# Two layer-norm stages of a fused two-layer kernel: statistics issued ahead of the tile's matmul pipe, and their sums taken by fp32 matmuls

## The reference

```python
# x = x + layernorm(L0_attn(layernorm(x)))
x_norm = _layernorm(x, ln1_g, ln1_b)
beta = x_norm @ w_in.T                              # 1024 -> 2 x 64
c_r, c_i = _chunked_eigenstate(log_decay, frequency, beta_r, beta_i)   # scan in chunks of 64
c_r = einsum('hjk,bthk->bthj', coupling, c_rh)      # 4 heads of 16 x 16, and the same for c_i
h = concat([c_r, c_i]) @ w_out.T
gate = sigmoid(x_norm @ w_gate.T + b_gate)
x1 = residual + gate * h
x2n = _layernorm(x1, ln2_g, ln2_b)
mlp = silu(x2n @ w_mlp1.T + b_mlp1) @ w_mlp2.T + b_mlp2   # 1024 -> 4096 -> 1024
return x1 + mlp
```

## Time and profile before

| | |
|---|---|
| runs of the kernel before | 9948.44 and 10145.99 us, median 10047.22 |
| the profiled execution | 9851.24 us |
| its span, slowest core (core 5) | 9849.6 us; the 8 cores 9819.1 to 9849.6 |
| busy in the span | PE 4153.1, PEld 2035.3, DVE 2423.2, ACT 1759.9, POOL 779.8 us |
| mean granted TensorE clock | 0.699 of 2.4 GHz |
| stages by time | L1A to about 1590 us, L1B to 3860, then L2A 5110, L2B 6210, L3 8655, L4 |

### The profile page before, as it was taken

The page is one execution under the profiler, slowest core; times in us unless marked ns, Lnnn a source line. Parts: engine busy times, 40 slices in busy tenths (PEclk is TensorE's granted clock), DMA queues, the critical chain, the costliest instruction groups (busy, mean ns, idle before and its releaser), DMA issues.

```text
span 9849.6 us, 65349 instructions; the slowest of 8 cores (9819.1 to 9849.6 us)
## 1 busy us (share of the span) xinstructions
PE 4153.1 (42%) x20436; PEld 2035.3 (21%) x20436; DVE 2423.2 (25%) x1874; ACT 1759.9 (18%) x2144; POOL 779.8 (8%) x517
## 2 busy tenths in 40 slices
PE   0332222555555552677645453233333333333443
PEld 0000002444444441233212121011111111110111
DVE  2233220111111111222211112233333333312122
ACT  0111111222222221121111111011111111122332
POOL 0332330000000000000000000111110001100000
PEclk9655556777777776888877676566666666666776
DMA  1000014000000003101131212100000000010000
GB/s 37 0 34 35 17 49 79 26 27 30 26 26 26 26 22 77 35 30 43 43 94 43 77 60 60 39 17 17 17 17 17 17 17 9 9 47 32 20 34 26
DMA packets 198078, 335.10 MB, mean 34 GB/s; under 512 B 3408, under 2 KB 114288, under 8 KB 195568
## 3 DMA queue, kind: packets, MB, share of 16 engines
q1 hardware_dynamic: 110992, 158.34, 4.7%
q10 hardware_dynamic: 82912, 120.59, 3.4%
q0 software_dynamic: 3840, 52.00, 3.0%
HBM read 262.24 MB, written 120.59 MB: 39 GB/s over the span
## 4 chain that ended last, share of the span: by engine, by line
PE 40%; DVE 22%; DMA 11%; ACT 10%; issue 9%; POOL 6%; DVEq 1%; another core or an unknown queue 1%; ACTq 0%; POOLq 0%; SPq 0%
PE ps1a L210 10%; PE ps1b L210 9%; PE ln_psQ L165 3%; PE ln_psS L165 3%; ACT ln_xb L310 3%; ACT ln_xb L299 3%; DVE ln_A L326 3%; PE ps2a L210 2%; PE ps2b L210 2%; PE ps41a L210 2%; DMA xt<-s_t 2%; PE psKa L210 2%; PE psKb L210 1%; DVEq L152 1%; PE psRa L210 1%
## 5 line engine op out<-in xcount | busy, mean ns | idle before, releaser
L315 DVE TENSOR_SCALAR ln_m<-ln_psS 128x512 f32<-128x512 f32 (+1 forms) x97 | 57.5, 592 | 4441.8 <-PE ln_psQ L165 4441.8
L165 PE MATMUL ln_psS<-ln_xb,c_ones 128*128 128x512 bf16 (+1 forms) x776 | 277.1, 534 | 1961.4 <-ACT ln_xb L299 1961.4
L165 PEld LDWEIGHTS ln_psS<-ln_xb,c_ones 128*128 128x128 bf16 x776 | 97.8, 135 | 2125.8 <-issue 2113.7
L210 PE MATMUL ps1a<-xn2b,w_s 128*128 128x256 bf16 x2304 | 320.1, 285 | 352.9 <-DMA s_t<-ao 308.4
L210 PE MATMUL psKa<-mixk,wk_s 128*128 128x512 bf16 x288 | 86.4, 452 | 837.1 <-DVE mixr L1010 837.1
L165 PE MATMUL ln_psQ<-ln_xb,c_ones 128*128 128x512 bf16 (+1 forms) x776 | 282.8, 544 | 351.0 <-ACT ln_xb L310 351.0
L210 PE MATMUL ps1a<-ht,wd_s 128*128 128x512 bf16 x864 | 211.3, 405 | 371.8 <-DMA xt<-s_t 274.5
L310 ACT ACTIVATE ln_xb<-ln_xb 128x4096 bf16<-128x4096 bf16 (+1 forms) x97 | 289.4, 2983 | 338.9 <-PE ln_psS L165 338.9
L210 PE MATMUL ps1a<-y2b,wg_s 128*128 128x512 bf16 x864 | 218.5, 399 | 264.7 <-DMA hq_t<-ht 245.9
L326 DVE RECIPROCAL ln_A<-ln_t 128x512 f32<-128x512 f32 (+1 forms) x97 | 267.6, 2759 | 188.6 <-ACT ln_t L324 188.6
L210 PE MATMUL ps1b<-xn2b,w_s 128*128 128x256 bf16 x2304 | 311.9, 280 | 2.7
(11 more groups left out here) (285 smaller groups left out, 7129.5 us busy)
## 6 DMA issues: line engine op xcount, KB each, us to landing
xt<-s_t SPq DMA_DIRECT2D x35, 2048.0 KB, 8.1
hq_t<-ht ACTq DMA_DIRECT2D x9, 3072.0 KB, 10.8
ht<-hq_t SPq DMA_DIRECT2D x9, 3072.0 KB, 11.6
xt<-xs SPq DMA_DIRECT2D x9, 2048.0 KB, 9.7
x_t<-y ACTq DMA_DIRECT2D x9, 2048.0 KB, 7.3
x1t<-x_t SPq DMA_DIRECT2D x18, 1024.0 KB, 5.3
xst<-xs SPq DMA_DIRECT2D x18, 1024.0 KB, 5.4
s_t<-ao ACTq DMA_DIRECT2D x18, 1024.0 KB, 4.7
```

The lines of the kernel that those rows point to most:

```text
L165: last = e.matmul(ps_ap, l, r, start=(i == 0), stop=(i == n - 1))
L210: last = e.matmul(ps_ap, l, r, start=(i == 0), stop=(i == n - 1))
L315: b.op("vector", lambda e: e.tensor_scalar(self.m[:, :n], self.psS[:, :n], inv, None, ALU.mult))
```

## The change

Four things are edited, all in L1A and L1B.

1. `stats` is cut in two: `statsA` (Copy, psS, Square, psQ) and `statsB` (the rest). Other stages still call both in a row.
2. L1A: `statsPart(t+1)` (statsA) is issued before `gatePipe(t)`; `applyPart(t+1)` (statsB and the rest of preA) stays where preA was. The coupling matmuls of preB go to psBr and psBi. The POOL multiply of yy is issued behind the last of the four DVE operations.
3. L1B: `postA(t-1)` and `preA_(t+1)` are issued before `pipe(t)`, `preRest(t+1)` and `postRest(t-1)` (statsB and what follows) behind it. The two have a scratch each (ln, lnP), and the squares go to h1b.
4. L1B: there is no Copy any more. psS takes fp32 matmuls straight from x1t or ao with a fp32 matrix of ones (c_onesf).

```diff
+    def statsA_f32(self, n, xten, sq, nch=NCHUNK, first=None):
+        b.mm(self.psS[:, :n], [(cst["onesf"][:, :], xten[:, c, :n]) for c in range(nch)],
+             extra=first)
+        psS_mark = b.val["tensor"]
+        b.op("scalar", lambda e: e.activation(
+            sq[:, 0:nch, :n], xten[:, 0:nch, :n], AF.Square, bias=0.0, scale=1.0),
+            after={"scalar": b.val["scalar"], "tensor": psS_mark}, extra=first)
+        b.mm(self.psQ[:, :n], [(cst["ones"][:, :], sq[:, c, :n]) for c in range(nch)])
...
-        b.op("gpsimd", lambda e, yy=yy: e.tensor_mul(yy[:, :, :], yy[:, :, :], AB))
         b.op("vector", lambda e, xb=xb: e.tensor_mul(xb[:, :, :], xb[:, :, :], gB))
         b.op("vector", lambda e, xb=xb: e.tensor_add(xb[:, :, :], xb[:, :, :], bB))
         applySnap[t] = b.now()
+        b.op("gpsimd", lambda e, yy=yy: e.tensor_mul(yy[:, :, :], yy[:, :, :], AB))
         b.mm(psBr[:, :], [(w_in_r[:, k, :], xb[:, k, :]) for k in range(8)])
...
-        b.mm(ln.psS[0:64, :], [(wcp[:, :], ct[:, 0:TT])])
+        b.mm(psBr[:, :], [(wcp[:, :], ct[:, 0:TT])])
...
     for t in range(NTILE):
+        if t + 1 < NTILE:
+            b.scope_push(base=applyEnd[t])
+            statsPart(t + 1)
+            b.scope_pop()
         gm = gatePipe(t, mmax(applySnap[t], gateEnd.get(t - 1), woEnd.get(t - 1),
                               {"sdma": stm[t - 2]} if t - 2 in stm else None))
...
         if t + 1 < NTILE:
-            b.scope_push(base=mmax(preASnap[t], preBEnd[t]))
-            preA(t + 1)
+            b.scope_push(base=mmax(statsEnd[t + 1], preBEnd[t]))
+            applyPart(t + 1)
             b.scope_pop()
...
     for t in range(NT):
-        pipe(t, mmax(preSnap[t], pipeEnd.get(t - 1),
+        if t - 1 >= 0:
+            b.scope_push(base=mmax(pipeEnd[t - 1], postEnd.get(t - 2)))
+            postA(t - 1)
+            b.scope_pop()
+        if t + 1 < NT:
+            b.scope_push(base=preEnd[t])
+            preA_(t + 1)
+            b.scope_pop()
+        pipe(t, mmax(preEnd[t], pipeEnd.get(t - 1),
                      {"sdma": stm[t - 2]} if t - 2 in stm else None))
         pipeEnd[t] = b.now()
         if t + 1 < NT:
-            b.scope_push(base=preSnap[t])
-            pre(t + 1)
+            b.scope_push(base=preAEnd[t + 1])
+            preRest(t + 1)
             b.scope_pop()
-            preSnap[t + 1] = b.now()
+            preEnd[t + 1] = b.now()
         loadx1(t + 2)
         if t - 1 >= 0:
-            b.scope_push()
-            post(t - 1)
+            b.scope_push(base=postAEnd[t - 1])
+            postRest(t - 1)
             b.scope_pop()
+            postEnd[t - 1] = b.now()
```

More of the change, by code:

```diff
@@ L158, in op, with mm @@
             self.scopes[-1]["seen"][key] = self.val[key]
-    def mm(self, ps_ap, pairs, after=None):
+    def mm(self, ps_ap, pairs, after=None, extra=None):
         def f(e):
@@ L166, in f @@
             return last
-        self.op("tensor", f, after=after)
+        self.op("tensor", f, after=after, extra=extra)
     def pipe(self, n, stages, guard=2, extra=None, start=None):
@@ L256, in emit_consts @@
     cst["ones"] = ones
+    onesf = b.sbuf("c_onesf", [128, 128], F32)
+    b.op("gpsimd", lambda e: e.memset(onesf[:, :], 1.0))
+    cst["onesf"] = onesf
     return cst
@@ L291, in mkcomp, with statsA @@
             self.A2 = self.b.sbuf("ln_A2", [128, self.nn], F32)
-    def stats(self, x_chunks, n, nch=NCHUNK, comp=False, first=None, x_all=None):
+    def statsA_f32(self, n, xten, sq, nch=NCHUNK, first=None):
         b, cst = self.b, self.cst
[L295 to L307, removed]
+        b.mm(self.psS[:, :n], [(cst["onesf"][:, :], xten[:, c, :n]) for c in range(nch)],
[5 more added lines that the diff above has]
+        b.mm(self.psQ[:, :n], [(cst["ones"][:, :], sq[:, c, :n]) for c in range(nch)])
+    def statsA(self, n, x_all, nch=NCHUNK, first=None):
+        b, cst = self.b, self.cst
+        b.op("scalar", lambda e: e.activation(
+            self.xb[:, 0:nch, :n], x_all, AF.Copy, bias=0.0, scale=1.0), extra=first)
         b.mm(self.psS[:, :n], [(cst["ones"][:, :], self.xb[:, c, :n]) for c in range(nch)])
@@ L551, in emit_l1a, with statsPart, applyPart @@
     bB = ln1b[:, :].unsqueeze(2).broadcast_to([128, NCHUNK, TT])
-    def preA(t):
+    def statsPart(t):
+        x = xt[t % 3]
+        ln.statsA(TT, x[:, :, :], first={"sync": ldm[t]})
+        statsEnd[t] = b.now()
+    def applyPart(t):
         nonlocal A2B
@@ L558, in preA @@
         bb = btb[t % 2]
-        ln.stats(None, TT, comp=True, first={"sync": ldm[t]}, x_all=x[:, :, :])
+        ln.statsB(TT, comp=True)
         if A2B is None:
@@ L590, in preB @@
         emit_eigenstate(b, eg, bb, ct, TT, ccol[:, 0:2], egs)
[L591 to L594 removed]
+        b.mm(psBr[:, :], [(wcp[:, :], ct[:, 0:TT])])
+        b.op("vector", lambda e, cp=cp: e.tensor_copy(cp[:, 0:TT], psBr[:, :]))
+        b.mm(psBi[:, :], [(wcp[:, :], ct[:, TT:2 * TT])])
+        b.op("vector", lambda e, cp=cp: e.tensor_copy(cp[:, TT:2 * TT], psBi[:, :]))
     def gatePipe(t, start):
@@ L700, in emit_l1b, with preA_, preRest @@
     bB = ln2b[:, :].unsqueeze(2).broadcast_to([128, NCHUNK, N])
-    def pre(t):
+    mPB = lnP.m[:, :N].unsqueeze(1).broadcast_to([128, NCHUNK, N])
+    APB = lnP.A[:, :N].unsqueeze(1).broadcast_to([128, NCHUNK, N])
+    def preA_(t):
+        ln.statsA_f32(N, x1t[t % 2], h1b[:, 0:8, :], first={"sync": ldm[t]})
+        preAEnd[t] = b.now()
+    def preRest(t):
         x1 = x1t[t % 2]
         xb = xn2b[t % 2]
-        ln.stats(None, N, x_all=x1[:, :, :], first={"sync": ldm[t]})
+        ln.statsB(N)
         b.op("vector", lambda e, x1=x1, xb=xb: e.tensor_sub(xb[:, :, :], x1[:, :, :], mB))
@@ L725, in pipe, with postA, postRest @@
         ], start=mmax(start, m1))
-    def post(t):
+    def postA(t):
+        lnP.statsA_f32(N, ao[t % 2], h1b[:, 8:16, :])
+        postAEnd[t] = b.now()
+    def postRest(t):
         xs = xst[t % 2]
         a = ao[t % 2]
-        ln.stats(lambda c, a=a: a[:, c, :], N, x_all=a[:, :, :])
-        b.op("vector", lambda e, a=a: e.tensor_sub(a[:, :, :], a[:, :, :], mB))
-        b.op("vector", lambda e, a=a: e.tensor_mul(a[:, :, :], a[:, :, :], AB))
+        lnP.statsB(N)
+        b.op("vector", lambda e, a=a: e.tensor_sub(a[:, :, :], a[:, :, :], mPB))
+        b.op("vector", lambda e, a=a: e.tensor_mul(a[:, :, :], a[:, :, :], APB))
         b.op("vector", lambda e, a=a, xs=xs: e.tensor_add(a[:, :, :], a[:, :, :], xs[:, :, :]))
```

47 lines of the change are left out of this document (34 added, 13 removed).

## The result

The changed kernel took 9719.64 us (median of 11 runs, 9631.09 to 10058.58) against 10066.96 us of the kernel before on the same chip (10 runs, 9865.56 to 10230.4); ratio 0.972, 95% interval 0.964 to 0.980: faster, and whether by the full 2% is left just open. The ratio goes by the six executions of 9631 to 9720 us and leaves out those in which the cores of one die ran over 1% longer at a lower granted clock. The profiled execution is the longest of the six, 9719.6 us; before it was 9851.2. The forecast was 9695, range 9590 to 9880.

What follows compares the result with a forecast made beforehand. The prediction took chains of waits inside one tile, with no engine filling any stage, to bound the kernel. From the profiled 9851.2 us it took 130 (L1A) and 26 (L1B) to reach 9695 us, range 9590 to 9880.

Steps and rivals of the forecast that it cites:

- L1A, -130: L1A: 154 us from an earlier Sqrt over 8 intervals, less 24 us for late loads in 6 intervals.
- Rival 4: L1A: late load delays the gate matmuls, half of the 19.3 gone in 6 tiles (10 us each); 9731 us, chance 0.07.
- the 19.3: L1A: the Sqrt starts 19.3 us earlier, at 1025.41 in place of 1044.70, in each of 8 intervals.
- L1B, the chain: L1B gap: both DVE chains stay in it, and postA's first matmul waits for the xs load, until 2801.0.
- L1B, -26: L1B: 1.7 us less in each of 15 steady gaps, 26 us, edges 0.5; between -85 and +40.
- F1: L1B gap: first psS set of eight fp32 matmuls, put at 6.0 us, about 5 us of it slow.
- F2: L1B gap: second psS set of eight fp32 matmuls, put at 5.1 us, 3.2 slow and 1.9 fast.
- the "9.0": L1B gap: twice the 4.5 us from the end of psS to the end of psQ, before the pipe starts.
- the forecast's own signs of being wrong: Wrong if psS starts before the xs load lands, a set takes under 4 or over 8 us, or later stages change length.
- Rival 1: L1B: fp32 sets bound by weight loads, F1 + F2 = 13.4, L1B +15 with edges; 9736 us, chance 0.14.
- Rival 2: L1A and L1B: clock stays high through F1 and F2, late load hidden, -154 - 85; 9612 us, chance 0.18.
- Rival 3: L1B: fp32 matmul costs 1.94 us whatever its width, 15.5 a set, +340; total 10035 us, chance 0.05.

Runs made afterwards that it cites:

- experiment 1: Changed kernel with the L1B of before put back, so L1A changed alone; ratio 0.984 against the kernel before, interval 0.971 to 0.997.
- experiment 5: Changed kernel with L1A's statistics of the next tile issued behind the gate's matmuls instead of ahead; one execution, 9639.4 us.
- experiment 6: Changed kernel with L1A's POOL multiply of yy issued behind the projections instead of ahead; ratio 0.969, interval 0.952 to 0.985.
- experiment 4: Changed kernel with postA's first matmul in L1B no longer waiting for the store and xs load of the tile before; median 9716.03 us.
- experiment 3: Changed kernel with the bf16 Copy and bf16 sums of before in L1B, in the new order; median 9774.06 us, no ratio.

## Why the prediction came out as it did

The time of the profiled execution, 9719.6, is 25 us from the forecast, but that nearness is in part luck: on core 5 the change is worth 211 us, not 156, and core 2, which sets the time, is 79 us longer (9717.2 - 9638.4): 14 in L1A and 66 in L1B, 45 of these in its four slow pipes and the rest in its gaps. Two misses of opposite sign nearly cancel. The other five executions behind the ratio took 9631 to 9693 us, nearer to core 5's span.

- *L1A, -130*: right in size and in mechanism. Measured -134 on core 5 and -131 alone (experiment 1). The Sqrt is late by nothing but ACT's output copies; the load is late and the gate's matmuls stand behind it (experiment 5: 25 us, the forecast had 24). The intervals bear out both terms one by one, 19 us without a late load and 15.9 with one. The POOL multiply gave nothing (the same intervals, and experiment 6). Rival 4, which had 10 us of the 19.3 gone in six tiles, is refuted: 3.4 were.
- *L1B, the chain*: right. PE's idle time ahead of postA is 39.9 us, forecast 40.2, and it is the xs load that ends it (experiment 4: store and load, 10 us a tile). The pipe's start still lies behind the DVE chains.
- *L1B, -26*: mis-sized; -82 was measured on core 5. The term that failed is the one for the four sets behind the idle time, F1 of 6.0, F2 of 5.1 and twice 1.87 in the "9.0", because the forecast had the clock at its lower level for about 5 us in each burst and psQ always slow. Measured from the groups: 5.75 + 4.13 + 2 x 1.24 = 12.4 against 14.8, so 2.5 us a tile less, and in the up-projection (632.0 - 602.9) / 18 = 1.6 instead of 0.8. Over 16 gaps and 18 pipes that is 40 + 14 = 54 of the missing 56 us. One of the forecast's own signs of being wrong, a set under 4 us, came true here: 3.62, which is its 3.6 for the higher clock.
- *Rival 1* (weight loads bind fp32): refuted. In the timeline a psS of fp32 at the higher clock took 3.62 us, four times 1.03 less the tail, and its loads fit beside it. Loads are longer, as the groups of weight loads of after, core 5, show:

```profile
L165 PEld LDWEIGHTS ln_psS<-x1t,c_onesf 128*128 128x128 f32 x269 | 56.4, 215 | 21.6 <-issue 12.4
L165 PEld LDWEIGHTS ln_psQ<-h1b,c_ones 128*128 128x128 bf16 x280 | 27.6, 107 | 110.0 <-issue 104.8
```

  215 ns against 107, yet 16 of them (3.4 us) lie beside matmuls of 3.6. The Trainium skill's rule that the fast weight load is off for FP32 (TensorE: Matmul & The Clock Gate, section "Weight-path perf modes") agrees with the loads; in this case it cost nothing.
- *Rival 2* (both sets fast, late load hidden, 9612): nearer in L1B (-85) than the forecast, and wrong in L1A. Its nearness in L1B is luck too: it had both psS at 3.6, where psS of ao took 5.75, and left psQ and the pipe's first sets slow, where they turned fast. *Rival 3* (price by instruction) is refuted: 5.75 and 4.13 us a set, not 15.5.
- The forecast did not ask whether fp32 sums were worth having in the moved order. By experiment 3 they weren't: 2.5 us a gap, since the first Copy with its bf16 psS takes less than the fp32 psS, and the second Copy is free.
- *What it left out*: that cores would differ among themselves. It covered this only by the room in its range.

## What to carry to other kernels

Where every step waits for all that was issued before it, moving the arithmetic is worth only what the last wait allows: here the sums moved, the Sqrts, the DVE chains and a load's wait did not, and a gap went from 61 to 57 us; moving the Sqrts and the DVE chains too and freeing the load made it 17 to 20. Follow the moved instruction's queue as well as the one it left: a Copy that is hoisted takes its load's wait along, and a Silu behind a hoisted Sqrt makes PE wait inside the pipe. Replacing an ACT pass by fp32 matmuls did not pay here, not even for the pass on the chain (5.7 us against 4.4); and a time that is the slowest of eight cores should be read by stage on several cores.
